# Layer 3 attention with q and k kept in fp32 on both halves of the partitions, and score products of 64 rows

## The reference

```python
H, Dh = 16, 64                       # x: [1, 2048, 128]
q = (x @ Wq).reshape(B, N, H, Dh).transpose(0, 2, 1, 3)
kv = x @ Wkv
k, v = the two halves of kv, in heads as q
s = jnp.einsum('bhid,bhjd->bhij', q * scale, k)
gm = max(s, axis=-1)                 # over all 2048 keys, masked or not
p = where(causal_mask, 0.0, exp(s - gm))
out = einsum('bhij,bhjd->bhid', p, v) / (sum(p, axis=-1) + EPS)
return out (heads side by side) @ Wo + bo
```

## Time and profile before

| | |
|---|---|
| time, three executions | 2102.0, 2104.84 (median), 2114.51 us |
| span of the profiled execution (first to last instruction) | 2102.4 us |
| its prologue of the attention, from the first products of v | 1076 to 1114.4 us |
| its loop over heads, from the first score product | 1114.4 to 2013 us (898.6 us) |
| busy in the loop: PE, DVE, POOL, ACT | 819.97, 752.94, 738.54, 703.49 us |
| mean share of the DMA engines in the loop | 0.92 |

### The profile page before, as it was taken

How to read it: one execution, slowest core, us unless ns; L and a number is a source line. 1 busy time by engine, 2 the same in 40 slices (tenths; PEclk the granted TensorE clock), 3 DMA queues, 4 the chain that set the end, 5 groups by cost and what they waited for, 6 DMA issues and landing times. The chain is left out here.

```text
span 2102.4 us, 30965 instructions
## 1 busy us (share of the span) xinstructions
PE 1735.7 (83%) x10655; PEld 1123.8 (53%) x10655; DVE 1409.2 (67%) x2076; ACT 1217.1 (58%) x2054; POOL 1136.2 (54%) x1025
## 2 busy tenths in 40 slices
PE   4637999999578587677888999899999989999958
PEld 2414777789443366443554555555555555555534
DVE  2474777773255588665248888888888888888821
ACT  3274333336247366234347777787778777777733
POOL 1053554532300376211335888888888888888850
PEclk9577999997589899897999999999999999999979
DMA  1212222220100000003214999999989899999960
GB/s 28 62 39 69 72 89 67 81 81 26 27 15 2 12 1 1 1 1 98 61 39 85 157 167 156 162 161 165 160 159 155 159 157 160 163 159 165 164 125 20
DMA packets 630968, 193.10 MB, mean 92 GB/s; under 512 B 591553, under 2 KB 622034, under 8 KB 630814
## 3 DMA queue, kind: packets, MB, share of 16 engines
q1 hardware_dynamic: 622342, 167.55, 44.1%
q0 software_dynamic: 8224, 23.51, 3.6%
q10 hardware_dynamic: 248, 0.06, 0.0%
HBM read 36.90 MB, written 12.48 MB: 23 GB/s over the span
## 5 line engine op out<-in xcount | busy, mean ns | idle before, releaser
L2849 DVE TENSOR_REDUCE half_max<-scores 128x1 f32<-128x1024 f32 x512 | 614.6, 1219 | 135.0 <-PE scores L2678 128.7
L2595 POOL TENSOR_TENSOR p_low<-p,p_high 128x2048 f16<-128x2048 f32 (+15 forms) x256 | 576.4, 2252 | 146.1 <-ACT p_high L2779 130.7
L2678 PE MATMUL scores<-k_high,q_pair 128*128 128x512 f16 x1024 | 303.6, 378 | 70.4 <-ACT p L2764 68.1
L2764 ACT ACTIVATE p<-scores,exp_bias 128x1024 f32<-128x1024 f32 (+7 forms) x384 | 317.7, 862 | 70.8 <-DVE exp_bias L2854 68.6
L2678 PE MATMUL scores<-k_low,q_pair 128*128 128x512 f16 x1024 | 304.2, 379 | 0.0
L2779 ACT ACTIVATE p_high<-p 128x2048 f16<-128x2048 f32 (+15 forms) x256 | 282.5, 1104 | 36.4 <-DMA pT_high<-p_high 31.2
L2698 PEld LDWEIGHTS scores<-v_pair,pT_high 128*128 128x128 f16 x2176 | 151.5, 98 | 104.4 <-issue 62.0
L2698 PE MATMUL scores<-v_pair,pT_low 128*128 128x129 f16 x2176 | 186.2, 222 | 10.6 <-DMA pT_low<-p_low 10.1
L2698 PE MATMUL scores<-v_pair,pT_high 128*128 128x129 f16 x2176 | 188.4, 222 | 5.2 <-DMA pT_high<-p_high 5.1
L2698 PEld LDWEIGHTS scores<-v_pair,pT_low 128*128 128x128 f16 x2176 | 146.9, 98 | 46.5 <-DMA pT_low<-p_low 15.5
L2678 PEld LDWEIGHTS scores<-k_low,q_pair 128*128 128x128 f16 x1024 | 99.1, 97 | 121.7
(11 more groups left out here) (488 smaller groups left out, 3241.3 us busy)
## 6 DMA issues: line engine op xcount, KB each, us to landing
pT_high<-p_high SPq DMA_TRANSPOSE x256, 3.6
pT_low<-p_low SPq DMA_TRANSPOSE x256, 3.7
slots<-zero_row SPq DMA_DIRECT2D x1, 3036.0 KB, 14.4
slot_rows<-slots SPq DMA_DIRECT2D x23, 132.0 KB, 2.4
slots_out<-expert_out SPq DMA_DIRECT2D x23, 128.0 KB, 1.8
w_up<-in_L_ffn_inter_w_dram SPq DMA_DIRECT2D x1, 2048.0 KB, 9.2
dispatched<-moe_rows SPq DMA_DIRECT2D x1, 1024.0 KB
slot_rows<-dispatched SPq DMA_DIRECT2D x4, 256.0 KB, 3.9
```

Source lines behind the costliest of these rows:

```text
L2595: pool.tensor_tensor(flat(pl[:, buf, b0:b0 + n, :]), flat(p32[:, buf, b0:b0 + n, :]), flat(ph[:, buf, b0:b0 + n, :]), ALU.subtract).then_i ...
L2678: mm = pe.matmul(ps[:, b.start + i, :], q, k[:, par, cs(2 * half + i)], start=start, stop=not start)
L2764: act.activation(flat(p32[:, buf, b0 + first:b0 + first + w, :]), flat(ps[:, banks(p, half), :])[:, 0:w * P], ACT.Exp, bias=bias[:, p:p + ...
L2849: dve.tensor_reduce(mx[:, p % 2, half:half + 1], flat(ps[:, b[half], :]), AX.X, ALU.max, negate=True)\
```

## The change

`q2` and `k2` take the place of `qs2`, `kh2` and `kl2`: fp32, with the same 64 rows on both halves of the partitions, as `project` leaves them. ACT's copy of a unit (`copy_unit`) now writes fp32 and alone sets `q_ready` or `k_ready`; DVE's `low` is gone. A half of the scores is two fp32 matmuls of 64 rows and 512 columns: the first 512 keys from partitions 0 to 63, the other 512 from partitions 64 to 127, each into a bank of its own. Room is made by laying `wv` (used in the prologue) into `p32` (used in the loop), and by leaving out the constant `pick`, which nothing reads.

```diff
@@ constants
-    m.pick = alloc("pick", [P, HD, P])
-                for t in (m.ident, m.head_ones, m.pick, m.ones, m.sum_pick):
+                for t in (m.ident, m.head_ones, m.ones, m.sum_pick):
-                pool.affine_select(out=m.pick[:].rearrange("p e (h d) -> p e h d", d=HD), ...
@@ layer3_attention
-            wq, wk, wv = sb("w_q2", [P, 2, 2, DH]), sb("w_k2", [P, 2, 2, DH]), sb("w_v", [P, H * DH])
+            wq, wk = sb("w_q2", [P, 2, 2, DH]), sb("w_k2", [P, 2, 2, DH])
-            qs2, kh2, kl2 = (sb(n, [P, 2, TOK], F16) for n in ("q_pair", "k_high", "k_low"))
+            q2, k2 = (sb(n, [P, 2, TOK]) for n in ("q_twice", "k_twice"))
+            wv = p32[:, 0, 0:H * DH // P, :].rearrange("p b c -> p (b c)")
@@ PE: unit_free, scores
-                        wait(pe, q_low if kind == "q" else k_lows, at(NCH, unit_count((u - 1) % PAIRS), 1 if u else 0))
+                        wait(pe, q_ready if kind == "q" else k_ready, at(NCH, unit_count((u - 1) % PAIRS), 1 if u else 0))
-                        q = qs2[:, par, ORDER[p] * P:(ORDER[p] + 1) * P]
-                        for k, start in ((kh2, True), (kl2, False)):
-                            for i in range(2):
-                                mm = pe.matmul(ps[:, b.start + i, :], q, k[:, par, cs(2 * half + i)], start=start, stop=not start)
+                        for i in range(2):
+                            rows = slice(i * DH, (i + 1) * DH)
+                            mm = pe.matmul(ps[:, b.start + i, :], q2[rows, par, ORDER[p] * P:(ORDER[p] + 1) * P],
+                                           k2[rows, par, cs(2 * half + i)], start=True, stop=True)
@@ ACT: copy_unit (high before)
-                            act.activation(qs2[:, par, cs(c)], ps[:, b, :], ACT.Copy, scale=SCALE).then_inc(q_high, 1)
+                            act.activation(q2[:, par, cs(c)], ps[:, b, :], ACT.Copy, scale=SCALE).then_inc(q_ready, 1)
-                            act.activation(kh2[:, par, cs(c)], ps[:, b, :], ACT.Copy).then_inc(k_highs, 1)
+                            act.activation(k2[:, par, cs(c)], ps[:, b, :], ACT.Copy).then_inc(k_ready, 1)
@@ DVE: low, and its calls in head (one in each iteration) and prologue (eight)
-                            dve.scalar_tensor_tensor(out=low_part, in0=ps[hi, b, :], scalar=SCALE, in1=low_part,
-                                                     op0=ALU.mult, op1=ALU.subtract).then_inc(q_low, 1)
-                            dve.tensor_tensor(kl2[:, par, cs(c)], ps[:, b, :], kh2[:, par, cs(c)], ALU.subtract)\
-                               .then_inc(k_lows, 1)
-                                if i and not last:
-                                    low(at, 1 - par, s, UBANK)
```

More of the change, by code:

```diff
@@ L116, in _ @@
                 pool.memset(m.hdiv[:], 1.0).then_inc(ones_set, 1)
-                pool.wait_ge(ones_set, 7)
+                pool.wait_ge(ones_set, 6)
                 pool.affine_select(out=m.ident[:], in_=m.ident[:], compare_op=ALU.is_equal, fill=0.0, base=0,
                                    pattern=[[-1, P]], channel_multiplier=1).then_inc(shaped, 1)
[L122 to L125, removed]
                 blocks = m.head_ones[:].rearrange("p (h d) -> p h d", d=HD)
@@ L129, in _ @@
                                    pattern=[[-HD, HEADS], [0, HD]], channel_multiplier=1).then_inc(shaped, 1)
-                pool.wait_ge(shaped, 3)
+                pool.wait_ge(shaped, 2)
                 pool.affine_select(out=blocks, in_=blocks, compare_op=ALU.is_ge, fill=0.0, base=HD - 1,
@@ L139, in _ @@
                 pool.wait_ge(picked, 1)
-                pool.wait_ge(shaped, 5)
+                pool.wait_ge(shaped, 4)
                 pool.tensor_tensor(m.sum_pick[:], m.sum_pick[:], m.head_ones[:].unsqueeze(1).to_broadcast([P, HD, P]), ALU.mult)\
@@ L173, in _ @@
                     dve.tensor_copy(m.cols[:, t * P:(t + 1) * P], turned[:, t, 0:P]).then_inc(cols_ready, 1)
-                dve.wait_ge(shaped, 6)
+                dve.wait_ge(shaped, 5)
                 dve.tensor_reduce(m.hmod[:], m.head_ones[:].rearrange("p (g i d) -> p i g d", g=4, i=4)[:, :, :, 0],
@@ L182, in _ @@
             def _(pe):
-                pe.wait_ge(shaped, 6)
+                pe.wait_ge(shaped, 5)
                 pe.wait_ge(rows_loaded, 16 * len(VECTORS))
@@ L2428, in layer3_attention @@
     BLOCKS = NT + 1
-    hi = slice(DH, P)
     UNITS = [("k", 0), ("k", 1), ("k", 2), ("k", 3), ("q", 0), ("q", 3), ("q", 1), ("q", 2)]
@@ L2512, in layer3_attention @@
             o_pair = ps[:, OBANK, :].rearrange("p (r c) -> p r c", r=2)
-            with stage(nc, "wv_loaded", "w_loaded0", "w_loaded1", "const_set", "q_raw", "k_raw", "v_raw", "q_high", "q_low", "k_highs",
-                       "k_lows", "v_high", "v_low", "v_copied", "scored", "half_maxed", "biased", "exped", "masked",
+            with stage(nc, "wv_loaded", "w_loaded0", "w_loaded1", "const_set", "q_raw", "k_raw", "v_raw", "q_ready", "k_ready", "v_high", "v_low", "v_copied", "scored", "half_maxed", "biased", "exped", "masked",
                        "p_high", "p_low", "hT0", "hT1", "hT2", "hT3", "lT0", "lT1", "lT2", "lT3",
                        "summed", "o_out", "den_set", "den_inverted", "o_summed", "o_ready") as (
-                    block, wv_loaded, w_loaded0, w_loaded1, const_set, q_raw, k_raw, v_raw, q_high, q_low, k_highs, k_lows, v_high, v_low,
+                    block, wv_loaded, w_loaded0, w_loaded1, const_set, q_raw, k_raw, v_raw, q_ready, k_ready, v_high, v_low,
                     v_copied, scored, half_maxed, biased, exped, masked, p_high, p_low,
@@ L2551, in prologue @@
                     def prologue(at):
-                        sp.dma_start(wv[:], inp["L3_attn_Wkv"][:, ds(H * DH, H * DH)]).then_inc(wv_loaded, 16)
+                        sp.dma_start(wv, inp["L3_attn_Wkv"][:, ds(H * DH, H * DH)]).then_inc(wv_loaded, 16)
                         load(0)
@@ L2670, in scores @@
                         if p == 0 and half == 1:
-                            wait(pe, k_lows, now(NCH, NCH))
-                            wait(pe, q_low, now(NCH, 2))
+                            wait(pe, k_ready, now(NCH, NCH))
+                            wait(pe, q_ready, now(NCH, 2))
                         if p == NT // 2 and half == 1:
-                            wait(pe, q_low, now(NCH, NCH))
-                        q = qs2[:, par, ORDER[p] * P:(ORDER[p] + 1) * P]
-                        for k, start in ((kh2, True), (kl2, False)):
-                            for i in range(2):
-                                mm = pe.matmul(ps[:, b.start + i, :], q, k[:, par, cs(2 * half + i)], start=start, stop=not start)
+                            wait(pe, q_ready, now(NCH, NCH))
+                        for i in range(2):
+                            rows = slice(i * DH, (i + 1) * DH)
+                            mm = pe.matmul(ps[:, b.start + i, :], q2[rows, par, ORDER[p] * P:(ORDER[p] + 1) * P],
+                                           k2[rows, par, cs(2 * half + i)], start=True, stop=True)
                         mm.then_inc(scored, 1)
@@ L2725, in prologue @@
                             project(at, 0, u, u % 8)
-                        pe.wait_ge(q_low, NCH)
+                        pe.wait_ge(q_ready, NCH)
                         for p in range(2):
@@ L2741, in _, with copy_unit @@
                 def _(act):
-                    def high(at, par, u, b):
+                    def copy_unit(at, par, u, b):
                         kind, c = UNITS[u]
@@ L2802, in head @@
                                 if i and not last:
-                                    high(at, 1 - par, s, UBANK)
+                                    copy_unit(at, 1 - par, s, UBANK)
                     def prologue(at):
@@ L2808, in prologue @@
                         for u in range(len(UNITS)):
-                            high(at, 0, u, u % 8)
+                            copy_unit(at, 0, u, u % 8)
                         act.wait_ge(v_low, 2 * NT)
@@ L2823, in _ @@
                 def _(dve):
[L2824 to L2829, removed]
-                            dve.scalar_tensor_tensor(out=low_part, in0=ps[hi, b, :], scalar=SCALE, in1=low_part,
-                                                     op0=ALU.mult, op1=ALU.subtract).then_inc(q_low, 1)
-                        else:
-                            wait(dve, k_highs, at(NCH, unit_count(u), 1))
-                            dve.tensor_tensor(kl2[:, par, cs(c)], ps[:, b, :], kh2[:, par, cs(c)], ALU.subtract)\
-                               .then_inc(k_lows, 1)
                     def values_low(n, g, b):
@@ L2877, in prologue @@
                             values_low(u // 2, u % 2, u % 8)
-                        for u in range(len(UNITS)):
-                            low(at, 0, u, u % 8)
                         for p in range(2):
```

## The result

The changed kernel takes 2140.86 us (median of four, 2138.52 to 2143.23), the kernel before beside it 2106.45: a ratio of 1.0162, with a 95% interval from 1.0139 to 1.0186. It is slower by 1.6%; 2332 us had been forecast, which is 11% slower, and the range began at 2150.

A forecast was written before the change was run, and what follows sets the result against it. PE was taken to bound the loop over heads for more than nine tenths. 2102.4 + 165 (score products) + 133 (turns) - 70 (waits) - 1 (small edits) = 2329.4; with 2.4 for median above span, 2332 us; range 2150 to 2460.

The forecast's parts named there:

- the order of the records: Score products: two lower-row records, then two upper-row ones, started in order; three slots a lone half, 165 us more.
- rival 2: Score products fully side by side, two by two, only the turns remaining: +63, 2168 us; chance 0.11.
- The turns: PE's changes between 64 and 128 rows, six an iteration: 1.04 us a pair, 133 us in the loop.
- The waits: PE's waits ahead of score products, nearly all for the exponential: the whole 70 us go.
- the waits for the transposes: PE's waits for transposes in the loop: 9 us, which stay.
- the chain of maxima, bias and exponential: Steps holding back score products, with the low part ahead of the maxima: some 3.7 us, no longer after the change.
- rival 5: Score products two by two and turns hidden; up to 70 us of waits go: 2035 to 2070 us; chance 0.04.
- a floor 72 us down: DMA engines' share of the loop, 0.92 of 898.6 = 827 us, taken to allow up to 70 us of gain.
- The small edits: Ahead of the loop the last low part goes, -0.7 us; fp32 copies, `pick` and the load of `wv`: nothing.

The follow-up runs named there:

- e1: Changed kernel with both products of a half taken from the same lower 64 rows; 2673.16 us in a single execution.
- e7: Changed kernel with the four products of the two neighbouring halves ordered lower, lower, upper, upper rows; 2177.74 us in a single execution.
- e2: Changed kernel with the unit put between the first two halves, so eight turns an iteration in place of six; 2175.93 us.
- e3: Changed kernel with the third and fourth half next to each other, so four turns an iteration in place of six; 2117.96 us.
- e5: Kernel before without DVE's low part in the loop, PE waiting for ACT's copy of the unit alone; 2105.16 us.
- e6: Changed kernel with DVE's low part put back, into a tile that nothing reads, and PE waiting for it before the next unit; 2148.76 us.
- e10: Changed kernel with most of the low transposes left out, one block of each tile's low parts turned; 2136.65 us.
- e4: Kernel before with PE's order of the four-turn run, having no turns itself; 2104.65 us, ratio 0.9987.
- e8: Kernel before with most of the low transposes left out, one block of each tile's low parts turned; 2068.17 us.

## Why the prediction was wrong

**The step that failed** is the order of the records: "if the queue is kept in order, B1 stands behind A2 and can only start with it. So A1 is alone". It was taken between two bounds of which the trace of before could tell neither, and it put 165 us into the sum, where the runs show none: a half takes the same two slots of 0.43 us as its four fp16 records did. `e1` shows that the products are side by side because of their rows, `e7` that a product waits to start only for its own rows, even behind four records for the others. The Trainium skill (TensorE: Matmul & The Clock Gate, "The mechanism") has matmuls start and end strictly in program order. For the starts that doesn't hold here: four slots in `e7` are only to be had if the third product starts ahead of the second. For the ends the late signal in `e7` agrees with it. What stands between the code's order and the array, a reordering of the records or two queues, the runs don't tell. With this term at nothing the prediction's own sum is its rival 2, some 2168 us.

**The turns** were rightly found in layer 2, and rightly named as the part that the diff doesn't tell. The size was 1.04 us a pair; it is 0.84. The turns into and out of the score products cost 0.19 to 0.20 on the score products' side, as read. The unit kept its 0.96. On the add-up's side the block behind the unit, which has a turn only at its end, grew from 0.64 to 0.74, the 0.09 that was charged; the two blocks with a turn at both ends grew by about 0.10 each too (to 0.75 for eleven products and 0.80 for twelve), where 0.19 each was charged. So, if the end costs the same in all three blocks, the 0.10 at the start of what comes, read between fp32 products, is missing at the start of the add-up's fp16 products; two of these are the 0.20 too much. The Trainium skill (TensorEngine Tiling (Array Packing), "Key Properties") states a drain at a change of the tiling mode; the trace agrees in that a turn has a price, 0.155 us by the iterations of `e2` and `e3`, but that the price is a drain isn't shown.

**The waits** went, 69 us for a forecast of 70, so with the measured turns rival 2 gives 2102.4 + 107.5 - 70 - 1 + 2.4 = 2141 us, the measured time. That the 69 meets the 70 is luck: only 53 of it are waits ahead of score products, and the waits for the transposes, which were to stay, fell too (15.2 to 5.7). The reason lay elsewhere as well. The prediction had the chain of maxima, bias and exponential freed of the low part, and in rival 5 the same 70 us as a gain if only the turns were free. `e5` is that case without turns, and it gains nothing: the transposes, which the prediction had put at a floor 72 us down by the DMA share of 0.92, were a bound already. By its own numbers the DMA engines, with 827 us, were as busy as PE, with 819.97. In the changed kernel the waits went because PE became slow enough to hide both the chain (`e6`: 8 us) and the transposes (`e10`: 4 us).

**The small edits** were as foretold: `pick` shows nowhere, and the loop starts 1.9 us earlier, for 0.7.

So the change pays with turns for something that brings nothing: it frees DVE, while the transposes bind. No version here that leaves nothing of the work out beats the kernel before by more than `e4`'s 0.13%; the changed kernel with four turns stays 0.5% above it.

Open is whether the transposes bind by SP, which issues them one after another, or by the DMA engines behind it: SP's rows fill nearly all of the time in the kernel before, but `e8` shortens them as well as the engines' share, and the rows don't tell what makes them long. The list of waits has SP waiting for its inputs for 175 us in that stretch, but by the timeline a high part's transpose starts, in the median, 6.0 us after ACT has written it.

## What to carry to other kernels

In this kernel products on different halves of the rows run side by side, but each change between them and products of all rows costs some 0.15 us on PE; count the changes in the loop, not the products, and put such products next to each other. Freeing an engine was worth nothing here while another resource stood close to the loop's length: before a share of 0.92 is called a floor, leave some of its work out and see whether the time falls. And where a trace can't tell between two bounds, test the likelier one in a small kernel: a value in between has no row behind it.

## What was not expected of the hardware

In `e1` the granted clock was at half, the 1.2 GHz level, from about 1125 to 1370 us of the run. PE had been busy for 4.82 of the 5 us from 1115 to 1120, still at 1.00, and from 1130 on it was busy all the time; then it rose to 1.00, the 2.4 GHz level, and stayed there to the end of the loop. Its stretches:

```profile
1115.00:1500.00 385.00, 383.73 (x1221) 169.22 (x1221) 136.53 (x157) 141.90 (x191) 141.09 (x107) 0.68 0.40 71
1150.00:1200.00 50.00, 50.00 (x116) 21.45 (x115) 13.32 (x16) 14.73 (x20) 12.91 (x12) 0.50 0.25 42
1300.00:1350.00 50.00, 50.00 (x125) 21.63 (x124) 13.32 (x15) 13.41 (x19) 14.07 (x10) 0.50 0.39 69
1400.00:1450.00 50.00, 50.00 (x253) 24.03 (x252) 24.62 (x28) 24.87 (x33) 25.33 (x19) 1.00 0.63 106
```

About half as many matmuls went through in 50 us as later (116 and 253). With a mean clock of 0.68 over 385 us some 123 us are lost, by our estimate. Some 17 of the changed kernel's 23 us of waits on PE go in exchange (PE waits for 6 us in `e1`), which leaves 106, about the 94 us by which this run stands above what its slots need. PE was doing the same score products, on the lower 64 rows alone, before and after the rise; it is one execution, and why the clock fell and rose isn't known.
